# xDeepFM-style scorer on one core: input split, deep-network input and output row placed elsewhere in the engines' orders

## The reference

```python
emb = tables[feat_idx, sparse]                                   # 512 x 26 x 32
linear_out = lin_sparse_w[feat_idx, sparse].sum(-1) + dense @ lin_dense_w
x0 = xk = emb
for w, bb in ((conv1_w, conv1_b), (conv2_w, conv2_b)):           # two CIN layers
    hp = einsum('bhd,bmd->bhmd', xk, x0).reshape(-1, h * M, E)
    xn = sigmoid(einsum('oi,bid->bod', w, hp) + bb)
    xk = xn[:, :half]; res.append(xn[:, half:])
cin_out = concat(res).sum(-1) @ cin_w + cin_b
deep_x = concat([emb.reshape(-1, M * E), dense])
h3 = tanh(tanh(tanh(deep_x @ W1 + b1) @ W2 + b2) @ W3 + b3)       # 845 -> 1024 -> 512 -> 256
return linear_out + cin_out + h3 @ deep_w + deep_b + bias[0]
```

## Time and profile before

| what | us |
|---|---|
| median of 3 runs | 430.91 |
| the profiled execution | 432.29 |
| its span (first to last instruction or DMA) | 430.4 |
| PE busy | 413.3 (96%) |
| DVE busy | 320.0 (74%) |
| ACT, POOL busy | 161.0, 167.3 |

### The profile page before, as it was taken

The page is one execution under the profiler, slowest core; times in us unless marked ns, Lnnn a source line. Parts: engine busy times, 40 slices in busy tenths (PEclk is TensorE's granted clock), DMA queues, the critical chain, the costliest instruction groups (busy, mean ns, idle before and its releaser), DMA issues. The chain is left out here.

```text
span 430.4 us, 5216 instructions
## 1 busy us (share of the span) xinstructions
PE 413.3 (96%) x1874; PEld 167.6 (39%) x1874; DVE 320.0 (74%) x356; ACT 161.0 (37%) x264; POOL 167.3 (39%) x146
## 2 busy tenths in 40 slices
PE   3978989999999999999999999999999999999997
PEld 1422323333333333333233333333333344886784
DVE  4115799898999799999798998998989895332121
ACT  3073252544544534535253544443543411111011
POOL 6663466664746584675540000000000193870000
PEclk9996999999999999999999999999999999999999
DMA  5357696888786898778887778675856720320000
GB/s 195 82 122 164 168 229 162 194 192 196 177 202 141 200 193 210 173 191 184 191 190 189 178 186 192 163 201 133 213 143 153 177 66 10 114 76 0 0 2 0
DMA packets 38304, 64.03 MB, mean 149 GB/s; under 512 B 19601, under 2 KB 22033, under 8 KB 38278
## 3 DMA queue, kind: packets, MB, share of 16 engines
q1 hardware_dynamic: 34694, 61.93, 58.3%
q0 software_dynamic: 3584, 1.76, 3.3%
HBM read 61.96 MB, written 1.71 MB: 148 GB/s over the span
## 5 line engine op out<-in xcount | busy, mean ns | idle before, releaser
L355 POOL DMA_INDIRECT emb<-in_table,rows x112 | 132.8, 1186 | 86.1 <-DMA emb<-in_table,rows 52.6
L730 DVE TENSOR_TENSOR prod<-ring,xk 128x1024 f32<-128x1024 f32 x112 | 132.7, 1217 | 29.2 <-PE ring L431 14.2
L730 DVE TENSOR_TENSOR copied<-copied,xk 128x1024 f32<-128x1024 f32 x96 | 115.4, 1242 | 0.5
L441 PE MATMUL conv<-prod,w_sb 128*64 128x512 f32 x448 | 112.2, 615 | 0.0
L441 PE MATMUL conv<-copied,w_sb 128*64 128x512 f32 x384 | 91.9, 594 | 1.5 <-DVE copied L730 1.5
L419 PE MATMUL conv<-sq,w_sb 117*64 117x512 f32 x384 | 88.1, 593 | 0.3 <-issue 0.3
L579 ACT ACTIVATE xk<-conv,const_sb 64x512 f32<-64x512 f32 x64 | 43.7, 683 | 97.2 <-PE conv L419 84.1
L376 POOL TENSOR_TENSOR xt_lo<-xt,xt_hi 128x512 fp32r<-128x512 f32 (+1 forms) x7 | 12.8, 1863 | 122.1 <-ACT xt_hi L640 122.1
L568 ACT ACTIVATE sq<-ring 117x512 f32<-117x512 f32 x90 | 48.6, 594 | 29.7 <-PE ring L403 23.5
L441 PEld LDWEIGHTS conv<-copied,w_sb 128*64 128x64 f32 x384 | 26.8, 137 | 57.6 <-issue 45.4
L419 PEld LDWEIGHTS conv<-sq,w_sb 117*64 117x64 f32 x384 | 27.2, 136 | 54.2 <-issue 53.4
(11 more groups left out here) (76 smaller groups left out, 299.2 us busy)
## 6 DMA issues: line engine op xcount, KB each, us to landing
copied<-laid SPq DMA_DIRECT2D x192, 256.0 KB
wpiece<-in_mlp SPq DMA_DIRECT2D x22, 256.0 KB
emb<-in_table,rows POOLq DMA_INDIRECT x112
raw<-laid SPq DMA_DIRECT2D x32, 52.0 KB
laid<-emb SPq DMA_DIRECT2D x16, 96.0 KB
sel_f<-in_sel SPq DMA_DIRECT2D x1, 832.0 KB, 5.7
const_sb<-in_const SPq DMA_DIRECT2D x1, 626.0 KB, 4.2
w_sb<-in_w SPq DMA_DIRECT2D x1, 416.0 KB, 6.3
```

Of the source, the lines that this page charges most:

```text
L355: pool.indirect_dma_start(out=emb[0:n, i, j, :], out_offset=None, in_=table, in_offset=bass.IndirectOffsetOnAxis(ap=rows[0:n, i, j:j + 1], ...
L441: mm = nc.tensor.matmul(conv[i % 2][c * HALF:(c + 1) * HALF, :], w2_sb[:, t, :], prod_of(r)[:, c, :], start=(t == 0), stop=(t == T2 - 1))
L730: nc.vector.tensor_tensor(prod_of(r)[:, :, :].rearrange("p c n -> p (c n)"), left[:, :, :].rearrange("p c n -> p (c n)"), xk[i % 2][:, :, ...
```

## The change

- **x** (`x_high`, `x_low`): fetch now makes four DMAs a pair, so that raw holds each chunk twice, in the partitions of the high part and of the remainder. ACT rounds all 122 partitions. DVE then does one `scalar_tensor_tensor` over 122 partitions, raw * m - x with m = 0 in the high rows and 1 in the remainder rows. The high rows become -x, and the 0/1 matrices carry the sign.
- **Pair 0 and 1**: ACT does `x_high(1)` between the sigmoids of pair 0's two chunks, and DVE does `x_low(1)` ahead of pair 0's first product (it was after its second). POOL no longer waits for gather 0 before it starts gather 1. On SP, LAY_AT is 1, and fetch comes ahead of copy k = 4. FOLD1_AT is 5 in all pairs.
- **Deep input**: the first 480 columns of xt_hi and xt_lo are made after pair 14's sigmoids of pair 15, and POOL's parts are held back to given products of pairs 14 and 15. The last 32 columns follow by themselves. deep(0, 0) moves to DEEP_AT = 2 and waits for all of xt_lo.
- **Output row**: the aux matmul moves to the start (WARM is 12), ACT copies its result to row_sb. The two folds are combined by DVE, and one matmul with two outputs (L588 of the changed kernel) gives the CIN part, which goes through ACT, SP and two DVE additions beside the deep layers. The last tile of layer 3 is computed in two halves of 256 columns, and so are the deep_w matmuls, the tanh and the last addition.

```diff
-LAY_AT = 3
-DEEP_AT = 1
+LAY_AT, FETCH_AT = 1, 4
+DEEP_AT = 2
-X_LOW_AT, TURN_AT, FOLD1_AT, PIECE_AT = (10, 5), 9, (5, 7), 11
-WARM = 13
+X_LOW_AT, TURN_AT, FOLD1_AT, PIECE_AT = (10, 5), 9, (5, 5), 11
+WARM = 12
...
 sync, fetch
-                    sp.wait_ge(x_lo_done, 2 * (i - RX + 1))
-                for c in range(2):
-                    sp.dma_start(raw[i % RX][HALF * c:HALF * c + M, :], laid[i, :, c * CH:(c + 1) * CH])\
+                    sp.wait_ge(x_lo_done, i - RX + 1)
+                for at in (0, XLO, HALF, HALF + XLO):
+                    c = at // HALF
+                    sp.dma_start(raw[i % RX][at:at + M, :], laid[i, :, c * CH:(c + 1) * CH])\
...
                 for k in range(NC):
                     n = NC * i + RC + k
+                    if k == FETCH_AT and i + RX < NPAIR:
+                        fetch(i + RX)
                     if n < NC * NPAIR:
                         copy(n)
                     if k == LAY_AT and i + RX < NPAIR:
                         lay_out(i + RX)
-                if i + RX < NPAIR:
-                    fetch(i + RX)
...
 gpsimd
-                if i:
+                if i >= 2:
                     pool.wait_ge(rows_in[(i - 1) % GSEM], ROWS * ((i - 1) // GSEM + 1))
...
+            pool.wait_ge(prod_done, T2 * (NPAIR - 2) + 12)
+            for k in range(3):
+                xt_low(k)
+            pool.wait_ge(prod_done, T2 * (NPAIR - 1) + 4)
+            for k in range(3, 5):
+                xt_low(k)
+            pool.wait_ge(prod_done, T2 * (NPAIR - 1) + 8)
+            for k in range(5, K1):
+                xt_low(k)
+            xt_low_rest()
...
 tensor
+            pe.wait_ge(aux_in, 16)
+            nc.tensor.matmul(conv[1][0:1, :], small_sb[:, C_AUX:C_AUX + 1], aux[:, :], start=True, stop=True)\
+              .then_inc(aux_done, 1)
...
-                    nc.tensor.matmul(row_ps[0:1, :], small_sb[:, C_AUX:C_AUX + 1], aux[:, :], start=True, stop=False)
-                    for k, col in enumerate((C_CIN1, C_CIN2)):
-                        for c in range(2):
-                            nc.tensor.matmul(by_c[:, c], small_sb[:, col + c:col + c + 1],
-                                             fold[:, k, :, :], start=False, stop=False, skip_group_check=True)
+                    nc.tensor.matmul(cin_ps, small_sb[:, C_ONE:C_ONE + 2], fold[:, 0, :, :], start=True, stop=True)\
+                      .then_inc(cin_done, 1)
+            deep_halves(2, MT[2] - 1)
...
+                for h in range(2):
+                    at = slice(h * BH, (h + 1) * BH)
+                    for k in range(kt):
+                        for j, (w, x_) in enumerate(((hi, xh), (lo, xh), (hi, xl))):
+                            mm = nc.tensor.matmul(half_bank[h], w[:, k, mt * P:(mt + 1) * P],
+                                                  x_[:, k, at], start=(k == 0 and j == 0),
...
 scalar
+            act.wait_ge(aux_done, 1)
+            nc.scalar.activation(row_sb[:, :], conv[1][0:1, :], ACT.Copy).then_inc(aux_read, 1)
             act.wait_ge(sel_done, 2)
             sigmoid(0, 0)
+            x_high(1)
             sigmoid(0, 1)
-            x_high(1)
...
 vector, x_low
-                for c in range(2):
-                    at = HALF * c
-                    nc.vector.tensor_tensor(x[i % RX][at + XLO:at + XK, :], raw[i % RX][at:at + M, :],
-                                            x[i % RX][at:at + M, :].bitcast(F32), ALU.subtract).then_inc(x_lo_done, 1)
+                nc.vector.scalar_tensor_tensor(x[i % RX][0:XEND, :], raw[i % RX][0:XEND, :],
+                                               small_sb[0:XEND, C_LOW:C_LOW + 1],
+                                               x[i % RX][0:XEND, :].bitcast(F32),
+                                               ALU.mult, ALU.subtract).then_inc(x_lo_done, 1)
...
                     if t == 0:
+                        if i == 0:
+                            x_low(1)
                         dve.wait_ge(xk_ready, 4 * (i + 1))
```

More of the change, by code:

```diff
@@ L182, in build @@
         HT = sum(MT)
+        XT = PB * (NPAIR - 1)
+        BH = B // 2
+        cin_ps = ring[2][0:2, 0, 0:NPAIR * CB]
+        half_bank = [MLP_BANKS[(HT - 1) % 2][:, 0:BH], ring[1][:, 0, 0:BH]]
+        row_half = [row_ps[0:1, 0:BH], ring[2][0:1, 1, 0:BH]]
         def piece(k):
@@ L311, in _ @@
             sp.dma_start(w2_sb[:, :, :], w2).then_inc(w2_in, 16)
+            sp.wait_ge(zeroed, 1)
+            sp.dma_start(aux[DENSE_AT:DENSE_AT + ND, :], dense_t).then_inc(aux_in, 16)
             lay_out(0)
@@ L465, in deep, with deep_halves @@
                 mm.then_inc(mlp_done, 1)
+            def deep_halves(layer, mt):
+                hi, lo, kt, xh, xl = deep_layers[layer]
+                n = sum(MT[:layer]) + mt
+                pe.wait_ge(tanh_done, n - 1)
+                for h in range(2):
[4 more added lines that the diff above has]
+                                                  x_[:, k, at], start=(k == 0 and j == 0),
+                                                  stop=(k == kt - 1 and j == 2))
+                    mm.then_inc(mlp_done, 1)
             pe.wait_ge(const_in, 16)
@@ L558, in x_high @@
                     act.wait_ge(spread_done, NS * (i - RX + 1))
-                nc.scalar.activation(x[i % RX][0:DENSE_AT, :], raw[i % RX][0:DENSE_AT, :], ACT.Copy)\
+                nc.scalar.activation(x[i % RX][0:XEND, :], raw[i % RX][0:XEND, :], ACT.Copy)\
                   .then_inc(x_hi_done, 1)
@@ L598, in _ @@
             act.wait_ge(zeroed, 1)
-            nc.scalar.activation(row_sb[0:1, 0:1], aux[0:1, 0:1], ACT.Sigmoid)
+            nc.scalar.activation(row_sb[0:1, 0:1], aux[0:1, 0:1], ACT.Sigmoid).then_inc(table_set, 1)
             act.wait_ge(const_in, 16)
@@ L646, in _ @@
             for layer, bias in enumerate((C_B1, C_B2, C_B3)):
-                for mt in range(MT[layer]):
+                for mt in range(MT[layer] - (1 if layer == 2 else 0)):
                     act.wait_ge(mlp_done, n + 1)
@@ L654, in _ @@
                     n += 1
+                if layer == 0:
+                    act.wait_ge(cin_done, 1)
+                    nc.scalar.activation(cin2[:, :, :], cin_ps.rearrange("p (i b) -> p i b", b=CB),
+                                         ACT.Copy).then_inc(cin_copied, 1)
+            for h in range(2):
+                at = slice(h * BH, (h + 1) * BH)
+                act.wait_ge(mlp_done, HT + h)
+                nc.scalar.activation(h3[:, 1, at], half_bank[h], ACT.Tanh,
+                                     bias=small_sb[:, C_B3 + 1:C_B3 + 2]).then_inc(tanh_done, 1)
         @block.vector
@@ L734, in _ @@
                     k = min(i, 1)
-                    if i == 0 and t == 1:
-                        x_low(1)
                     if t == X_LOW_AT[k] and i + 2 < NPAIR:
@@ L789 @@
     for at in (0, XLO, HALF, HALF + XLO):
-        sel1[at + first, pair_of] = 1
-        sel1[at + second, pair_of] = 1
+        sign = 1 if at % HALF else -1
+        sel1[at + first, pair_of] = sign
+        sel1[at + second, pair_of] = sign
         for m in range(M):
-            sel2[at + m, m // 2, m % 2, :] = 1
+            sel2[at + m, m // 2, m % 2, :] = sign
     fix = np.zeros((NPR, M), f32)
```

109 lines of the change are left out of this document (74 added, 35 removed).

## The result

The changed kernel takes **428.46 us** (median of 4 runs, 427.68 to 429.03) where the kernel before took 431.12 beside it (4 runs, 430.17 to 431.36): ratio 0.9941, 95% interval 0.9918 to 0.9964. It is faster, by 2.7 us where 8.5 were forecast; 422.4 and its range up to 427.0 are missed. The profiled execution took 429.03, span 427.2 for 430.4.

A forecast was written before the change was run, and what follows sets the result against it. PE, busy 413.3 of 430.4 us, was taken as the bound. Gains of 5.7 + 0 + 0.4 + 2.2 + 0.2 = 8.5 us took the median from 430.91 to 422.4 us, range 420.0 to 427.0.

The forecast's parts named there:

- Pair 1's x ahead of pair 0's products: Start, pairs 0 and 1: x of pair 1 ready sooner shrinks PE's hole; gain 5.7 us, bounds 3.0 to 7.0.
- lay_out of pair 1 comes 1.3 us sooner, at 24.55: Start, SP: gather 1 no longer waits for gather 0, so lay_out comes at 24.55 for 25.86.
- the hole only shrinks: Rival at the start: raw(1) lands above 31, the clock may fall; gain 3.0 for 5.7, 425.1 us, chance 0.17.
- the 4.9 up to layer 1: Start: layer 1 of pair 1 begins at 38.7 for 43.59, a gain of 4.9 us.
- the 0.8 behind it: Layer 1 of pair 1 to its turn: one x_low less should close a 0.6 us gap; gain 0.8 us.
- Neither is near the 4.1 us ... so I expect the clock to stay at 1.00: Start, PE: idle times of 1.7 and 1.2 us are too short for the granted clock to fall.
- my replay: Start, step by step: raw lands at 29.9, PE starts at 31.3, layer 1 of pair 1 at 38.7.
- Steady pairs: Pairs after the start: PE bounds them at 20.00 us each, so less DVE work gains 0.
- slower: Rival: copies held behind SP's waits come too late in every pair; 433.6 us, chance 0.04.
- Deep input: Pair 15: fewer POOL and DVE collisions, later deep(0, 0); gain 0.4 us, bounds 0.8 and a loss of 1.0.
- Output row: Between layers 1 and 2: 2.68 us of matmuls go, one of 0.43 plus 0.1 comes; gain 2.2 us.
- Tail: Last tile to end: halves lose 0.15 us, last addition falls from 0.68 to 0.35; net gain 0.2 us.

The follow-up runs named there:

- e4: The changed kernel with POOL's wait for gather 0 put back before gather 1: 427.93 us, ratio 0.9908.
- e2: The changed kernel with SP's lay_out and fetch of pair 1 ahead of copies 0 and 1: 426.65 us, ratio 0.9899.
- e1: The changed kernel with pair 1's x_high and x_low back behind pair 0's second xk and second product: 428.39 us, ratio 0.9929.
- b1: The kernel before with only SP's new order inside a pair, still two DMAs a fetch and two subtractions: 429.56 us, ratio 0.9967.
- e10: The changed kernel with output row, last tile and 13 warm-ups as before: 430.99 us, ratio 0.9993.
- e5: The changed kernel with e2's edit and one unread matmul in each of PE's two holes there: 424.82 us, ratio 0.9847.
- e7: The changed kernel with SP's old order inside a pair, keeping the four-DMA fetch: 432.59 us, ratio 1.0027.
- e0: The changed kernel itself, unedited, measured again as a base: 428.90 us, ratio 0.9931.
- e9: e5 with the old form of x (two DMAs a fetch, 96 partitions rounded, two DVE subtractions): 427.09 us, ratio 0.9906.

## Why the prediction was wrong

- **"Pair 1's x ahead of pair 0's products", 5.7: measured 0.4.** This step failed, in two links. The first is the landing of gather 1, "lay_out of pair 1 comes 1.3 us sooner, at 24.55": it came at 26.37. I moved the landing of a gather with its start, and e4 shows that the start doesn't matter: the gather landed behind the copies that SP had queued meanwhile, and with these behind it lay_out came at 23.10 (e2). With raw at 32.0 the new order gained and lost the same (e1). I had this as the rival "the hole only shrinks", raw above 31 with the xk behind it, and gave it 3.0 us and a chance of 0.17; even that was too good, since it left out that the products come 3 us later. Of the 5.7, the 4.9 up to layer 1 became a loss of 0.45; the 0.8 behind it came (17.51 to 16.66), but not for the reason given: b1, which still has two subtractions, shows 16.66 too.
- **"Neither is near the 4.1 us ... so I expect the clock to stay at 1.00".** This is the second link, and it would have failed by itself. The 4.1 us was one case and no limit: the clock fell 2.1 us after PE's last work in the changed kernel, 3.4 us in e10, 4.1 us before. In e2, with holes like those of my replay, it fell in the profiled run, and two of four runs took 4 us more. e5, with a hole of 0.43 us left, kept 1.00 in five runs. What decides when it falls the runs don't show.
- The rest of the replay (0.63 for x_high, 0.75 measured for the 0.70 of x_low, 38.7 for layer 1 and 55.4 for the turn) is confirmed by e5, 38.56 and 55.21, once the copies are moved and the holes filled, which the changed kernel doesn't do.
- **"Steady pairs: 0": measured -1.1.** Wrong in size and in reason. SP's order removes a wait for raw that the old kernel had in nearly every pair (b1), and without it the changed kernel takes 3.7 us more (e7). One clean pair was taken for all. The rival "slower", copies held back behind waits on SP, did not come true.
- **"Deep input", 0.4: measured -0.6.** Inside the bound of 1.0. The collisions went nearly as said (2.86, 2.35 and 2.54 a pair for 2.35), but DVE was still late for PE, and deep(0, 0), moved back, no longer covers it: it started 14.6 us after the first spreads where some 14 were forecast. I had counted DVE's chain to the last product and not PE's waits on the way.
- **"Output row", 2.2: right**, 2.15 in the trace; e10, which also undoes the halves, gives 2.1 to 2.7.
- **"Tail", 0.2: half right.** The halves cost 0.11 for 0.15. Matmuls of 256 columns start 0.12 us apart, each with a load of 128 columns that is shown as 0.19, so the loads hide. By the rule of the Trainium skill's TensorE: Matmul & The Clock Gate (Part 3, The mechanism), loads of one row group don't overlap, and it would be 5.1 us by the estimate made from it; the 2.87 us of the row decide against it. The same section also lets a load into the background weight buffer go ahead of running matmuls, which would fit the row; no run here shows which buffer a load uses. What follows the tile shrank by 0.21, not 0.35: an addition of 256 columns takes 0.41, and the two are one behind the other. Net 0.1.

Of the 8.5, 5.3 are missing at the start and 1.0 in pair 15, 0.1 in the output row and 0.1 in the tail, and 1.1 came in the steady pairs: -3.2 by the spans. The medians say 2.7 (and 2.4 by e0); the traced execution of the kernel before lay 1.4 us over its median, and I had taken all of that to lie outside the terms, which nothing shows.

## What to carry to other kernels

Moving a consumer ahead is worth nothing until its data are there: first ask what is queued in the DMA engines between the issue and the landing, and move the small transfer that the start waits for ahead of the bulk ones on the issuing queue (e2). A step that waits for a DMA, put ahead of a step that everything needs, turns its lateness into everybody's. Where PE must stand for a microsecond or two at the start, an unread matmul in the hole cost nothing measurable (from x_low's end to the sums of pair 1 it is 0.15 us in e2 and in e5) and kept the clock and the time in place in all five runs of e5, though not quite in e9. And the waits of one engine are read over all pairs, by line, before a term is booked at zero.

## What the runs showed of the hardware

- The granted clock can fall after two holes of 1.3 and 1.4 us, and two runs of four took 4 us more with a lower mean clock (e2). In one long hole it fell 2.1, 3.4 and 4.1 us after PE's last work (after, e10, before). The run with a mean clock lower by 0.012 took 3.6 us more (e0).
- The gather's landing is set by what else is in the DMA engines: 3.77 us after its last issue with 1 MB of copies queued from 18.82 on, 1.31 without; a start 1.2 us sooner changed nothing (e4).
- One `scalar_tensor_tensor` over 122 partitions and 512 columns, two operands in SBUF, takes 0.75 us, hardly more than the 0.70 of a `tensor_tensor` over 26 partitions.
